# The block scale of x computed by GpSimd, directly ahead of its multiplication by the reciprocal

## The chip, the cores and the metric

The kernel runs on one core of a Trainium2 chip. The metric is the device time of one execution in microseconds (us), as a median over runs of the same kernel. Five engines work side by side and wait for one another only through semaphores: TensorE (PE in the profile, its weight loads PEld), VectorE (DVE), ScalarE (ACT), GpSimd (POOL) and the queue that issues DMAs (SP). Each engine works through its own list of instructions in order, and an instruction that waits holds up all that stand behind it on that engine.

## What is computed

A layer of attention with rotary positions and a decay mask, then a gated feed-forward part whose inputs and weights are quantised to FP4 in blocks of 16 values, each part with a residual and a layer norm. The part on which the change bears is the quantisation:

```python
def fp4_quant_dequant(x):
    xb = x.reshape(shape[:-1] + (shape[-1] // BLOCK, BLOCK))      # BLOCK = 16
    scale = jnp.max(jnp.abs(xb), axis=-1, keepdims=True) / 6.0
    scale = jnp.maximum(scale, jnp.float32(1e-12))
    xn = xb / scale
    idx = jnp.searchsorted(_MID, jnp.abs(xn))
    q = _GRID[idx] * jnp.sign(xn) * scale
    return q.reshape(shape)
...
x = _layernorm(x + attention(x), axis=-1)
gate = fp4_linear(x, w_gate); y = fp4_linear(x, w_up)
h = silu(gate) * y
x = _layernorm(x + fp4_linear(h, w_down), axis=-1)
```

x is 8 batches of 1024 rows of 256, so a row has 16 blocks. Everything is float32.

## The kernel before

**Tiles and steps.** The 8 x 1024 rows are 64 tiles of 128 rows. After an opening written out by hand, a loop runs `step(s)` for s = 3 to 62, and a closing part is written out by hand again. Every engine has its own `step`, with its own order. Step s works on several tiles at once, one stage apart: `now` = s (scores and softmax), `prev` = s - 1 (attention output, first norm, quantisation of x up to `x_units`), `gu` = s - 2 (rest of the quantisation of x, then gate and up product), `dn` = s - 3 (gated unit, quantisation of h), `fin` = s - 4 (down product), `end` = s - 5 (second norm, output). Nothing schedules this at build time: the order in the text of each `step` is the order on the engine.

**Five kinds of step.** Each batch b has 8 steps (s = 8b + j), and the branches of `step` follow what is done for the next batch on top of the tile's work. A *rotation step* (j = 0, and 2, 4, 6 while there is a next batch) has TensorE project queries or keys into the PSUM tile `ps_g` (`project_next`). A *values step* (j = 3) and the *urgent step* (j = 7) project the values. A *plain step* (j = 1 and 5) has no projection. The steps 57 to 62 are those of the *last block*, with nothing for a next batch. Over the steps 3 to 62 there are 7 urgent, 7 values, 13 plain, 27 rotation steps and 6 of the last block. Urgent steps are followed by a rotation step, plain steps too, values steps too.

**The quantisation of x.** For tile i, `x_max` (L1588, VectorE) writes the largest magnitude of each block into row 2 of the small tile `xsc`; `x_scales` (L1595, VectorE) makes the scale from it in row 0; `x_reciprocals` (L1600, VectorE) writes the reciprocal in row 1; `x_units` (L2068, GpSimd) multiplies the 256 columns of x by it; ScalarE takes magnitudes (`x_magnitude`), VectorE rounds (`x_shift`, `x_grid`), GpSimd multiplies by the scale (`x_quantised`), TensorE transposes (`x1_transposes`). Helpers hold the instruction itself, so the profile shows L1454 for `x_max`, L1459 for `x_scales`, L1463 for `x_reciprocals` and L2019 for all multiplications by a scale.

**What stands around it.** On VectorE, behind `x_reciprocals(prev)`: `second_residual(fin)` (L1586) in the urgent and plain steps, then `h_low(dn, 0)` and `h_low(dn, 1)` (L1518, L1521), then the next step's `gated` and `silu` (L1468, L1479) of two thirds of the gated unit. On GpSimd, ahead of `x_units(prev)`: both halves of `decay_half(now)` (L2116) in the urgent and values steps; the first half only, with the second behind, in the plain steps and those of the last block; and none, with `h_quantised(dn, 1)` (L2019) ahead, in the rotation steps. Behind it come the copies of the rotated queries or keys (`rotated_low`, L2033 and L2035) in the urgent and plain steps.

**What TensorE waits for.** `prob_transposes(prev, g)` needs the decayed half and `htl_done` of `h_low` two steps of the pipeline back (the tile whose `h_low` ran in the step before). `project_next` and `values_next` wait, in `projection()`, until the last `silu` of tile `dn` is done (`h_done`), since `ps_g` holds that tile's gate and up product. `values_product_first(prev)` needs `probs_low(prev, 0)` (L1529).

Of the kernel before, what the change touches and what calls it, by code (L numbers as in the profile page):

```python
# [7 lines left out]
ALU = mybir.AluOpType  # L8
# [28 lines left out]
TIES_DOWN = 1.0 + 2.0 ** -22  # L37
MIN_SCALE = 1e-12
# [26 lines left out]
def live(i):  # L65

    return 0 <= i < TILES


def wait(eng, sem, value):  # L70

    if value > 0:
        eng.wait_ge(sem, value)
# [34 lines left out]
def build(nc, x, xt, wq, wk, wv, wg, wu, wd, decay, rope, ident_in, out):  # L108
# [4 lines left out]
    with ExitStack() as ctx:  # L113
# [1229 lines left out]
        def _(dve):  # L1343
# [248 lines left out]
                    wait(dve, xq_done, i)  # L1592
                    block_max(x1[:, i % 4, :], xsc, xmax_done)

            def x_scales(i):  # L1595
                if live(i):
                    wait(dve, xmax_done, i + 1)
                    block_scales(xsc, xscale_done)

            def x_reciprocals(i):  # L1600
                if live(i):
                    wait(dve, xscale_done, i + 1)
# [118 lines left out]
            weight_low(7)  # L1721
            x_max(0)
            weight_low(8)
            x_scales(0)
            x_reciprocals(0)
            row_max(2)
            probs_low(1, 0)
# [8 lines left out]
            silu(0, 0)  # L1736
            first_norm(1)
            x_max(1)
            x_scales(1)
            x_reciprocals(1)  # L1740

            def step(s):
                now, prev, gu, dn, fin = (s - lag for lag in range(5))
                rot, c_v = rotation(s), values_chunk(s)
                if rot is not None:
# [18 lines left out]
                    row_max(now)  # L1764
                    first_norm(prev)
                    x_max(prev)
                    x_scales(prev)
                    x_reciprocals(prev)
                    gated(gu, 0)
                    second_residual(fin)  # L1770
# [3 lines left out]
                elif c_v is not None and rotation_is_urgent(s):  # L1774
# [20 lines left out]
                    first_norm(prev)  # L1795
                    silu(gu, 0)
                    x_max(prev)
                    x_scales(prev)
                    x_reciprocals(prev)
                    second_residual(fin)  # L1800
                    h_low(dn, 0)
# [1 line left out]
                elif c_v is not None:  # L1803
                    if s > OPEN:
                        x_shift(gu)
                    row_inverse(prev)
                    gated(dn, 1)
                    gated(dn, 2)
                    silu(dn, 1)
                    silu(dn, 2)  # L1810
                    if s == OPEN:
                        x_shift(gu)
                    x_grid(gu)
                    probs_low(prev, 0)
                    h_max(dn)
                    h_scales(dn)
                    h_reciprocals(dn)
                    probs_low(prev, 1)
                    v_low(c_v, 0)
                    xqt_low(gu)  # L1820
                    v_low(c_v, 1)
                    h_shift(dn)
                    h_grid(dn)
                    first_residual(prev)
                    row_max(now)
                    gated(gu, 0)
                    silu(gu, 0)
                    first_norm(prev)
                    second_residual(fin)
                    x_max(prev)  # L1830
                    x_scales(prev)
                    x_reciprocals(prev)
                    h_low(dn, 0)
                    h_low(dn, 1)
                elif s // NT == NB - 1:
                    gated(dn, 1)
                    gated(dn, 2)
                    silu(dn, 1)
                    silu(dn, 2)
                    x_shift(gu)  # L1840
                    h_max(dn)
                    probs_low(prev, 0)
                    h_scales(dn)
                    x_grid(gu)
                    h_reciprocals(dn)
                    probs_low(prev, 1)
                    row_max(now)
                    xqt_low(gu)
                    row_inverse(prev)
                    first_residual(prev)  # L1850
                    h_shift(dn)
                    h_grid(dn)
                    gated(gu, 0)
                    first_norm(prev)
                    x_max(prev)
                    x_scales(prev)
                    silu(gu, 0)
                    second_residual(fin)
                    x_reciprocals(prev)
                    h_low(dn, 0)  # L1860
                    h_low(dn, 1)
                else:
                    gated(dn, 1)
                    silu(dn, 1)
                    row_inverse(prev)
                    x_shift(gu)
                    gated(dn, 2)
                    x_grid(gu)
                    silu(dn, 2)
                    h_max(dn)  # L1870
                    probs_low(prev, 0)
                    h_scales(dn)
                    h_reciprocals(dn)
                    probs_low(prev, 1)
                    xqt_low(gu)
                    row_max(now)
                    first_residual(prev)
                    h_shift(dn)
                    h_grid(dn)
                    first_norm(prev)  # L1880
                    x_max(prev)
                    gated(gu, 0)
                    x_scales(prev)
                    silu(gu, 0)
                    x_reciprocals(prev)
                    second_residual(fin)
                    h_low(dn, 0)
                    h_low(dn, 1)
# [23 lines left out]
            x_max(last - 1)  # L1912
            gated(last - 2, 0)
            silu(last - 2, 0)
            x_scales(last - 1)
            x_reciprocals(last - 1)
            row_inverse(last)
            h_low(last - 3, 0)
# [15 lines left out]
            last_moments_of(0, r1, (r1_done, TILES))  # L1934
            last_first_norm()
            x_max(last)
            x_scales(last)
            x_reciprocals(last)
            h_shift(last - 2)
            h_grid(last - 2)  # L1940
# [35 lines left out]
        def _(pool):  # L1976
# [86 lines left out]
            def x_quantised(i):  # L2063
                if live(i):
                    wait(pool, xgrid_done, i + 1)
                    times_scale(xv[:], xv[:], xsc, 0).then_inc(xq_done, 1)

            def x_units(i):  # L2068
                if live(i):
                    wait(pool, xinv_done, i + 1)  # L2070

                    wait(pool, xqt_done, i)
                    if i == 0:
                        pool.wait_ge(wquant_done, 3)
                    times_scale(xv[:], x1[:, i % 4, :], xsc, 1).then_inc(xn_done, 1)
# [92 lines left out]
            r1_variance(0)  # L2168
            r1_inverse(0)
            new_x_low(2)  # L2170
            x_units(0)
            rotated_low(0, 1)
            x_quantised(0)
# [1 line left out]
            decay_half(2, 1)  # L2175
            r1_variance(1)
            r1_inverse(1)
            x_units(1)
            rotate(1, 2, 0)

            def step(s):
                now, prev, gu, dn, fin, end = (s - lag for lag in range(6))
                rot, turned, c_v, c_x = rotation(s), rotation(s - 1), values_chunk(s), split_chunk(s)
                if rot is not None:
# [8 lines left out]
                    h_quantised(dn, 0)  # L2193
                    h_copied(dn)
                    h_quantised(dn, 1)
                    x_units(prev)
                    decay_half(now, 0)
                    decay_half(now, 1)
                elif c_v is not None and rotation_is_urgent(s):
# [10 lines left out]
                    r1_inverse(prev)  # L2210
                    decay_half(now, 0)
                    decay_half(now, 1)
                    x_units(prev)
                    rotated_low(*turned)
                elif c_v is not None:
# [11 lines left out]
                    r1_inverse(prev)  # L2227
                    decay_half(now, 0)
                    decay_half(now, 1)
                    x_units(prev)  # L2230
                elif s // NT == NB - 1:
                    r2_variance(end)
# [9 lines left out]
                    h_copied(dn)  # L2242
                    h_quantised(dn, 1)
                    decay_half(now, 0)
                    x_units(prev)
                    decay_half(now, 1)
                    if turned is not None:
                        rotated_low(*turned)
                else:
# [12 lines left out]
                    h_quantised(dn, 0)  # L2262
                    h_quantised(dn, 1)
                    decay_half(now, 0)
                    x_units(prev)
                    decay_half(now, 1)
                    if turned is not None:
# [14 lines left out]
            h_quantised(last - 3, 1)  # L2282
            r2_shift(last - 5)
            decay_half(last, 0)
            x_units(last - 1)
            decay_half(last, 1)
            x_quantised(last - 1)
            h_units(last - 2)
            last_inverse(0)
            x_units(last)  # L2290
            r2_variance(last - 4)
            r2_inverse(last - 4)
# [76 lines left out]
```

## Time and profile before

| | |
|---|---|
| median of 3 runs | 1030.45 us (1030.28 to 1030.70) |
| span of the profiled execution | 1028.9 us |
| granted TensorE clock | 1.00 |
| busy: PE, PEld, DVE, ACT, POOL | 98%, 89%, 87%, 57%, 73% of the span |
| `x_scales` on VectorE | 64 instructions, 26.9 us in all |
| `x_reciprocals` | 64 instructions, 15.9 us in all |
| `x_units` on GpSimd | 64 instructions, 39.9 us in all |

The span runs from the first to the last instruction of one execution; the runs' median is 1.55 us above it. A share of busy time is an average over stages with different limits; which wait ends last at a given place is read from the timeline of that place.

In a timeline row the columns are: start and duration in us, engine, line, operation, output<-input, shapes, number of instructions merged into the row, and in brackets the engine's idle time ahead of it with the engine and instruction that ended it. A row of two merged instructions has one start and the duration of both.

### The profile page before, as it was taken

To read this page: it belongs to the slowest core of one execution; us is meant where nothing else is said; L and a number is where in the kernel's file an instruction comes from. 1 tells how busy PE (TensorE), PEld (TensorE's weight loads), DVE (VectorE), ACT (ScalarE), POOL (GpSimd) and SP (SyncE) were. 2 spreads that over 40 slices of the span, in tenths; PEclk is the share of its full clock that TensorE was granted. 3 is DMA by queue.
4 is the path that set the end of the run, shared out by engine and by line. 5 is a ranking of instruction groups with operands and counts; after the bars stand their busy time and mean duration, and the time that the engine had idled before them with its cause. 6 is when DMAs were issued, how large, how long until landed. Compare 5 with 4: busy or idle time off the path is not lost.

```text
span 1028.9 us, 20101 instructions
## 1 busy us (share of the span) xinstructions
PE 1009.9 (98%) x6490; PEld 917.9 (89%) x6490; DVE 894.9 (87%) x1876; ACT 582.5 (57%) x1451; POOL 752.7 (73%) x973
## 2 busy tenths in 40 slices
PE   8899999999999999999999999999999999999996
PEld 7788999999999999999999999999999999989885
DVE  7989988888888889898888988889888888988886
ACT  3655556655665655655565665566556565565543
POOL 5977868776786867778687686876768686776654
PEclk9999999999999999999999999999999999999999
DMA  8020111110120101201020010211112020000000
GB/s 304 11 68 7 62 41 54 42 62 12 42 82 12 62 22 33 82 21 58 16 83 32 22 62 17 78 42 25 49 41 79 15 63 17 17 21 22 21 11 26
DMA packets 28263, 47.23 MB, mean 46 GB/s; under 512 B 2816, under 2 KB 21504, under 8 KB 26240
## 3 DMA queue, kind: packets, MB, share of 16 engines
q1 hardware_dynamic: 27472, 44.90, 13.8%
q8 instruction: 53, 0.87, 0.4%
q10 hardware_dynamic: 688, 1.05, 0.3%
q14 instruction: 50, 0.41, 0.1%
HBM read 37.55 MB, written 8.39 MB: 45 GB/s over the span
## 4 chain that ended last, share of the span: by engine, by line
PE 85%; POOL 5%; DVE 5%; issue 4%; DMA 1%; ACT 0%; SPq 0%; POOLq 0%; DVEq 0%; ACTq 0%
PE ps_g L491 11%; PE ps_g L492 11%; PE ps_g L493 11%; PE ps_oy L491 9%; PE ps_oy L493 9%; PE ps_oy L492 9%; PE ps_t L500 9%; PE ps_s L491 5%; PE ps_s L492 5%; PE ps_s L493 5%; POOL h L2019 2%; PE ps_oy L500 1%; DMA first_gate_up<-w_up 1%; PE ps_oy L677 1%; PE ps_oy L676 1%
## 5 line engine op out<-in xcount | busy, mean ns | idle before, releaser
L2019 POOL TENSOR_TENSOR h<-h,hsc 128x704 f32<-128x704 f32 x252 | 202.4, 815 | 58.8 <-DVE h L1511 28.5
L2116 POOL TENSOR_TENSOR prob<-prob,decay_t 128x512 f32<-128x512 f32 x128 | 163.6, 1292 | 4.0 <-ACT prob L1058 3.6
L491 PE MATMUL ps_oy<-v_h,pt_h 128*128 128x256 f32 x512 | 150.5, 294 | 0.0
L491 PE MATMUL ps_g<-wgu_h,xqt_h 128*128 128x480 f32 (+1 forms) x380 | 149.6, 394 | 0.4 <-DVE xqt_l L1548 0.3
L493 PE MATMUL ps_oy<-v_h,pt_l 128*128 128x256 f32 x512 | 144.8, 283 | 0.0
L492 PE MATMUL ps_oy<-v_l,pt_h 128*128 128x256 f32 x512 | 144.8, 283 | 0.0
L493 PE MATMUL ps_g<-wgu_h,xqt_l 128*128 128x480 f32 (+1 forms) x380 | 142.6, 375 | 0.0
L492 PE MATMUL ps_g<-wgu_l,xqt_h 128*128 128x480 f32 (+1 forms) x380 | 142.6, 375 | 0.0
L491 PE MATMUL ps_s<-k_h,q_h 128*128 128x512 f32 x256 | 104.8, 409 | 0.0
L491 PEld LDWEIGHTS ps_oy<-v_h,pt_h 128*128 128x128 f32 x512 | 97.7, 191 | 3.3 <-DVE pt_l L1529 1.7
L492 PE MATMUL ps_s<-k_l,q_h 128*128 128x512 f32 x256 | 100.6, 393 | 0.0
L493 PE MATMUL ps_s<-k_h,q_l 128*128 128x512 f32 x256 | 100.3, 392 | 0.0
L1007 ACT ACTIVATE th<-ps_g 128x240 f32<-128x240 f32 x188 | 68.1, 366 | 55.1 <-PE ps_g L493 52.3
L492 PEld LDWEIGHTS ps_oy<-v_l,pt_h 128*128 128x128 f32 x512 | 97.9, 191 | 1.4
L493 PEld LDWEIGHTS ps_oy<-v_h,pt_l 128*128 128x128 f32 x512 | 97.8, 191 | 0.0
L1015 ACT CAST pt_h<-ps_t 128x512 fp32r<-128x512 f32 x128 | 71.0, 589 | 38.2 <-PE ps_t L500 35.4
L1047 ACT CAST xqt_h<-ps_oy 128x256 fp32r<-128x256 f32 x63 | 23.6, 374 | 119.4 <-PE ps_oy L500 119.1
L1529 DVE TENSOR_TENSOR pt_l<-ps_t,pt_h 128x512 fp32r<-128x512 f32 x128 | 85.8, 671 | 5.1 <-ACT pt_h L1015 5.0
L491 PE MATMUL ps_oy<-wd_h,ht_h 128*128 128x256 f32 x315 | 89.1, 283 | 0.6 <-DVE ht_h L1521 0.6
L2025 POOL TENSOR_TENSOR rot_a<-rot_a,rot_b 128x512 f32<-128x512 f32 x58 | 75.0, 1294 | 19.6 <-DVE rot_b L1442 19.6
L493 PE MATMUL ps_oy<-wd_h,ht_l 128*128 128x256 f32 x315 | 89.2, 283 | 0.0
L492 PE MATMUL ps_oy<-wd_l,ht_h 128*128 128x256 f32 x315 | 89.2, 283 | 0.0
(260 smaller groups left out, 3053.7 us busy)
## 6 DMA issues: line engine op xcount, KB each, us to landing
rope_t<-rope SPq DMA_DIRECT2D x15, 1024.0 KB, 5.3
xres<-x SPq DMA_DIRECT2D x64, 128.0 KB, 2.0
out<-yout SPq DMA_DIRECT2D x63, 128.0 KB, 1.7
xin<-x_t SPq DMA_DIRECT2D x14, 512.0 KB, 4.1
first_rope<-rope SPq DMA_DIRECT2D x2, 512.0 KB, 8.4
decay_t<-decay SPq DMA_DIRECT2D x1, 960.0 KB, 12.2
first_down<-w_down SPq DMA_DIRECT2D x1, 704.0 KB, 10.3
first_gate_up<-w_gate SPq DMA_DIRECT2D x2, 256.0 KB, 7.8
```

The costliest lines, as they stand in the source:

```text
L491: pe.matmul(dst, a_h, b_h, start=(start and i == 0), stop=False)
L492: pe.matmul(dst, a_h, b_l, start=False, stop=False)
L493: mm = pe.matmul(dst, a_l, b_h, start=False, stop=(stop and i == n - 1))
L500: mm = pe.transpose(dst[:, i, 0:r], src, ident[0:r, 0:r])
L676: pe.matmul(ps_y[:, 0:D], ht_h[:, FC - 1, :], wd_h[:, FC - 1, :], start=False, stop=False)
L1007: nc.scalar.activation(th[:, part(r)], gate_up_at(i, r)[:, 0], ACT.Tanh, scale=0.5)\
L1015: nc.scalar.copy(pt_h[:, 4 * g:4 * g + 4, :], ps_t[:, g]).then_inc(pth_done, 1)
L1047: nc.scalar.copy(xqt_h[:], xqt_at(i)).then_inc(xqth_done, 1)
L1529: tt(pt_l[:, 4 * g:4 * g + 4, :], ps_t[:, g], pt_h[:, 4 * g:4 * g + 4, :].bitcast(F32), ALU.subtract).then_inc(ptl_done, 1)
L2019: return tt(blocks(dst), blocks(src), sc[:, which, at:at + n].unsqueeze(2).to_broadcast([P, n, QB]), ALU.mult)
L2025: tt(rot_a[:, a, :], rot_a[:, a, :], rot_b[:, 1 - a, :], ALU.add if a else ALU.subtract)\
L2116: tt(prob[:, keys], prob[:, keys], decay_t[:, lo:lo + CW], ALU.mult).then_inc(decayed, 1)
```

## The change

`x_scales(i)` moves from VectorE's program to GpSimd's. It becomes one `tensor_scalar` of 128 x 16 on GpSimd that waits for `xmax_done` and raises `xscale_done`. VectorE's `x_reciprocals` keeps its place behind `x_max` and still waits for `xscale_done`, which now comes from the other engine. On GpSimd the new instruction stands directly ahead of `x_units`, which waits for the reciprocal, in all 64 tiles. Nothing else is moved; TensorE's and ScalarE's lists are the same.

```diff
@@ VectorE
-            def x_scales(i):
-                if live(i):
-                    wait(dve, xmax_done, i + 1)
-                    block_scales(xsc, xscale_done)
-
             def x_reciprocals(i):
                 if live(i):
                     wait(dve, xscale_done, i + 1)
@@ VectorE, step, urgent branch (and the call taken out of every other branch)
                     x_max(prev)
-                    x_scales(prev)
                     x_reciprocals(prev)
@@ GpSimd
+            def x_scales(i):
+                if live(i):
+                    wait(pool, xmax_done, i + 1)
+                    nc.gpsimd.tensor_scalar(xsc[:, 0, :], xsc[:, 2, :], TIES_DOWN / 6.0, MIN_SCALE * TIES_DOWN, ALU.mult,
+                                            ALU.max).then_inc(xscale_done, 1)
+
@@ GpSimd, step, urgent branch (and ahead of x_units in every other branch)
                     decay_half(now, 0)
                     decay_half(now, 1)
+                    x_scales(prev)
                     x_units(prev)
                     rotated_low(*turned)
```

How the lists stand at two places. First the urgent step (s = 23). VectorE before; `xsc` is the tile of block scales, the row of L1459 is `x_scales`, and L1518 is `h_low`:

```order
L1454 TENSOR_REDUCE xsc<-x 128x16 [waits xq_done,x1_done]
L1459 TENSOR_SCALAR xsc<-xsc 128x16 [waits xmax_done]
L1463 RECIPROCAL xsc<-xsc 128x16 [waits xscale_done]
L1586 TENSOR_TENSOR r<-ps_oy,x 128x256 [waits y2_done,y_done]
L1518 TENSOR_TENSOR ht_l<-ps_t,ht_h 128x512 [waits hth_done]
```

VectorE in the changed kernel, same place:

```order
L1454 TENSOR_REDUCE xsc<-x 128x16 [waits xq_done,x1_done]
L1463 RECIPROCAL xsc<-xsc 128x16 [waits xscale_done]
L1586 TENSOR_TENSOR r<-ps_oy,x 128x256 [waits y2_done,y_done]
L1518 TENSOR_TENSOR ht_l<-ps_t,ht_h 128x512 [waits hth_done]
L1518 TENSOR_TENSOR ht_l<-ps_t,ht_h 128x128 [waits hth_done]
```

GpSimd in the changed kernel in the same step (`prob<-prob,decay_t` are the decay halves, `xv<-x,xsc` is `x_units`):

```order
L2081 TENSOR_TENSOR rs<-ve,mhalf 128x1 [waits x1_done,ve1_done]
L2108 TENSOR_TENSOR prob<-prob,decay_t 128x512 [waits exp_done] x2
L2057 TENSOR_SCALAR xsc<-xsc 128x16 [waits xmax_done]
L2005 TENSOR_TENSOR xv<-x,xsc 128x256 [waits xqt_done,xinv_done]
L2019 TENSOR_TENSOR k_l<-rot_a,k_h 128x512 [waits kqh_done]
```

The scale has gone from VectorE's list, and on GpSimd it stands behind both decay halves; VectorE's reciprocal, with everything behind it, waits for that place in GpSimd's list.

Second, GpSimd in a plain step (s = 25), before:

```order
L2019 TENSOR_TENSOR h<-h,hsc 128x192 [waits hcopy_done,hgrid_done]
L2116 TENSOR_TENSOR prob<-prob,decay_t 128x512 [waits exp_done]
L2019 TENSOR_TENSOR xv<-x,xsc 128x256 [waits xqt_done,xinv_done]
L2116 TENSOR_TENSOR prob<-prob,decay_t 128x512 [waits exp_done]
L2035 TENSOR_TENSOR q_l<-rot_a,q_h 128x1024 [waits kqh_done]
```

and in the changed kernel:

```order
L2005 TENSOR_TENSOR h<-h,hsc 128x192 [waits hcopy_done,hgrid_done]
L2108 TENSOR_TENSOR prob<-prob,decay_t 128x512 [waits exp_done]
L2057 TENSOR_SCALAR xsc<-xsc 128x16 [waits xmax_done]
L2005 TENSOR_TENSOR xv<-x,xsc 128x256 [waits xqt_done,xinv_done]
L2108 TENSOR_TENSOR prob<-prob,decay_t 128x512 [waits exp_done]
L2021 TENSOR_TENSOR q_l<-rot_a,q_h 128x1024 [waits kqh_done]
```

Here it stands behind the first decay half, and the second half has both the scale and the reciprocal's return ahead of it.

## Rows read from the trace of the kernel before

**Rows 1.** The page's first part: busy time of each engine

```profile
PE 1009.9 (98%) x6490; PEld 917.9 (89%) x6490; DVE 894.9 (87%) x1876; ACT 582.5 (57%) x1451; POOL 752.7 (73%) x973
```

**Rows 2.** Timeline, steps 23 and 24 (urgent, then rotation): DVE, POOL, PEld

```profile
385.83 0.26 DVE L1463 RECIPROCAL xsc<-xsc 128x16 f32<-128x16 f32 x1
...
386.27 0.87 DVE L1518 TENSOR_TENSOR ht_l<-ps_t,ht_h 128x512 fp32r<-128x512 f32 x2
...
386.96 0.63 POOL L2019 TENSOR_TENSOR xv<-x,xsc 128x256 f32<-128x256 f32 x1
...
388.11 0.70 DVE L1479 SCALAR_TENSOR_TENSOR h<-th,ps_g 128x240 f32<-128x240 f32 x2
...
388.99 0.19 PEld L491 LDWEIGHTS ps_g<-xt_h,wqkv_h 128*128 128x128 f32 x1
```

**Rows 3.** The tile view of xsc: count, shortest, median and longest duration (ns)

```profile
L1459 DVE TENSOR_SCALAR xsc<-xsc x64: 175/242/1267, 53.6 to 1000.0; 128x16 f32<-128x16 f32 x64
```

**Rows 4.** Timeline, a values step (s = 27): POOL and DVE

```profile
445.07 2.53 POOL L2116 TENSOR_TENSOR prob<-prob,decay_t 128x512 f32<-128x512 f32 x2
...
446.37 1.27 DVE L1459 TENSOR_SCALAR xsc<-xsc 128x16 f32<-128x16 f32 x1
```

**Rows 5.** Groups by line of POOL: busy us, mean ns of one, idle before

```profile
L2019 POOL TENSOR_TENSOR h<-h,hsc 128x64 f32<-128x64 f32 x63 | 18.5, 293 | 0.2 <-DVE h L1511 0.2
...
L2082 POOL TENSOR_SCALAR ve<-sq 128x1 f32<-128x1 f32 x63 | 12.0, 190 | 57.5 <-ACT ps_oy L1075 57.4
```

**Rows 6.** Timeline, a rotation step (s = 26): POOL

```profile
429.37 0.62 POOL L2019 TENSOR_TENSOR xv<-x,xsc 128x256 f32<-128x256 f32 x1 [0.40 <-DVE xsc L1463]
```

**Rows 7.** Timeline, steps 3 and 4: DVE, POOL, PEld

```profile
79.10 0.25 DVE L1463 RECIPROCAL xsc<-xsc 128x16 f32<-128x16 f32 x1
79.27 0.82 DVE L1518 TENSOR_TENSOR ht_l<-ps_t,ht_h 128x512 fp32r<-128x512 f32 x2
...
80.23 0.63 POOL L2019 TENSOR_TENSOR xv<-x,xsc 128x256 f32<-128x256 f32 x1
...
81.05 0.69 DVE L1479 SCALAR_TENSOR_TENSOR h<-th,ps_g 128x240 f32<-128x240 f32 x2
...
81.80 0.19 PEld L491 LDWEIGHTS ps_g<-xt_h,wqkv_h 128*128 128x128 f32 x1 [0.72 <-DVE h L1479]
```

**Rows 8.** Timeline, steps 25 and 26 (plain, then rotation): DVE, POOL, PEld

```profile
414.42 0.24 DVE L1463 RECIPROCAL xsc<-xsc 128x16 f32<-128x16 f32 x1
...
415.35 0.62 POOL L2019 TENSOR_TENSOR xv<-x,xsc 128x256 f32<-128x256 f32 x1
...
415.57 0.89 DVE L1518 TENSOR_TENSOR ht_l<-ps_t,ht_h 128x512 fp32r<-128x512 f32 x2 [0.64 <-ACT ht_h L1108]
...
417.42 0.69 DVE L1479 SCALAR_TENSOR_TENSOR h<-th,ps_g 128x240 f32<-128x240 f32 x2
...
418.30 0.19 PEld L491 LDWEIGHTS ps_g<-xt_h,wqkv_h 128*128 128x128 f32 x1
```

**Rows 9.** Timeline, the last block (steps 57, 59 and 60): DVE, POOL, PE

```profile
907.47 0.89 DVE L1518 TENSOR_TENSOR ht_l<-ps_t,ht_h 128x512 fp32r<-128x512 f32 x2 [0.34 <-ACT ht_h L1108]
...
933.44 0.23 DVE L1463 RECIPROCAL xsc<-xsc 128x16 f32<-128x16 f32 x1
...
934.70 0.63 POOL L2019 TENSOR_TENSOR xv<-x,xsc 128x256 f32<-128x256 f32 x1
...
934.73 0.89 DVE L1518 TENSOR_TENSOR ht_l<-ps_t,ht_h 128x512 fp32r<-128x512 f32 x2 [1.05 <-ACT ht_h L1108]
...
938.32 0.68 DVE L1529 TENSOR_TENSOR pt_l<-ps_t,pt_h 128x512 fp32r<-128x512 f32 x1
...
939.05 0.39 PE L491 MATMUL ps_oy<-v_h,pt_h 128*128 128x256 f32 x1
```

**Rows 10.** Waits of PE: us in total, times, longest

```profile
PE ps_t L500 <- POOL h L2019: 2.7, 5, 1.1
PE ps_oy L491 <- DVE ht_h L1521: 0.6, 1, 0.6
```

**Rows 11.** Busy time by stretch: PE, PEld, DVE, ACT, POOL, then granted clock

```profile
24.00:32.00 8.00, 5.31 (x34) 4.29 (x34) 7.58 (x15) 5.51 (x8) 7.29 (x6) 1.00 0.01 1
```

More of the change, by code:

```diff
@@ L1723, in _ @@
             weight_low(8)
-            x_scales(0)
             x_reciprocals(0)
@@ L1738, in _ @@
             x_max(1)
-            x_scales(1)
             x_reciprocals(1)
@@ L1797, in step @@
                     x_max(prev)
-                    x_scales(prev)
                     x_reciprocals(prev)
@@ L1830, in step @@
                     x_max(prev)
-                    x_scales(prev)
                     x_reciprocals(prev)
@@ L1855, in step @@
                     x_max(prev)
-                    x_scales(prev)
                     silu(gu, 0)
@@ L1882, in step @@
                     gated(gu, 0)
-                    x_scales(prev)
                     silu(gu, 0)
@@ L1914, in _ @@
             silu(last - 2, 0)
-            x_scales(last - 1)
             x_reciprocals(last - 1)
@@ L1936, in _ @@
             x_max(last)
-            x_scales(last)
             x_reciprocals(last)
@@ L2170, in _ @@
             new_x_low(2)
+            x_scales(0)
             x_units(0)
@@ L2177, in _ @@
             r1_inverse(1)
+            x_scales(1)
             x_units(1)
@@ L2212, in step @@
                     decay_half(now, 1)
+                    x_scales(prev)
                     x_units(prev)
@@ L2229, in step @@
                     decay_half(now, 1)
+                    x_scales(prev)
                     x_units(prev)
@@ L2244, in step @@
                     decay_half(now, 0)
+                    x_scales(prev)
                     x_units(prev)
@@ L2264, in step @@
                     decay_half(now, 0)
+                    x_scales(prev)
                     x_units(prev)
@@ L2284, in _ @@
             decay_half(last, 0)
+            x_scales(last - 1)
             x_units(last - 1)
@@ L2289, in _ @@
             last_inverse(0)
+            x_scales(last)
             x_units(last)
```

## The prediction, made before the changed kernel ran

> **What bounds the kernel now.** I read the page's busy line first [rows 1]: TensorE is busy for 1009.9 of 1028.9 us. VectorE has 87% and GpSimd 73%, so nothing gets faster by relieving them unless TensorE waits for them, and it hardly does: in the view of waits TensorE's largest single entry is 2.7 us for GpSimd, VectorE's largest after the opening 0.6 us [rows 10]. Any time that the change takes from TensorE is therefore lost for good, and little can be won. So I went to the timeline at the ends of the steps and asked, for each kind of step, how late the reciprocal comes and who is behind it.
>
> **What is removed.** VectorE loses 64 `tensor_scalar` of 128x16. They took 0.18 us at the shortest, 0.24 in the median and 1.27 at the longest [rows 3]. The long ones are holds: in a values step `x_scales` starts at 446.37 and ends at 447.64, 0.04 us behind the end of GpSimd's decay halves, 445.07 + 2.53 = 447.60 [rows 4]. The Trainium skill, "SBUF — State Buffer", § Who interferes with whom, says that a VectorE `tensor_scalar` in its fast mode and a GpSimd instruction exclude each other for the whole instruction; the trace agrees with that. By the rule alone the removal would hand all these holds back to VectorE.
>
> The rows say that it does not. The new instruction stands on GpSimd at the place where GpSimd comes free, so VectorE's reciprocal waits for the same end, and for a whole instruction more.
>
> **What is added.** One GpSimd `tensor_scalar` of 128x16 per tile, of which the trace has none. The nearest rows are the same operation on one column, 0.19 us, and a multiplication of 64 columns, 0.29 us [rows 5]. I take 0.21, near the first, since 16 columns are closer to 1 than to 64. The Trainium skill, "GPSIMD Engine Reference", § 4.1 Engine selection, puts elementwise work on VectorE, GpSimd being about 2x slower for two inputs; no run here shows this size. With twice VectorE's 0.24 the new instruction would cost 0.48, and the sum below would be some 9 us larger.
>
> The handover from GpSimd to VectorE is new. In the other direction it takes 0.08 (reciprocal's end to `x_units` at 429.37, whose 0.40 of idle time it ends [rows 6]); I take 0.04, between 0 and 0.08. So where GpSimd is busy until then, **the reciprocal starts 0.21 + 0.04 = 0.25 us behind the place where `x_units` starts now**.
>
> **Urgent step, 7 times.** `x_units` starts at 386.96, the reciprocal at 385.83 [rows 2]. It moves to 386.96 + 0.25 = 387.21, **1.38 later**. Behind it VectorE has no idle time: `h_low` at 386.27 follows back to back, and the two `silu` of the next step end at 388.11 + 0.70 = 388.81. They move to 390.19. TensorE's projection into `ps_g` waits for them; it starts at 388.99 now. How long that handover takes is seen at step 4, where TensorE does wait: the `silu` pair ends at 81.05 + 0.69 = 81.74 and the weight load starts at 81.80, 0.06 later [rows 7]. So the projection moves to 390.25, and TensorE loses 390.25 - 388.99 = **1.26 us**. The transposes ahead of it wait for `h_low` too, but for less, and inside the same delay. 7 x 1.26 = 8.8 us.
>
> **Plain step, 13 times.** The reciprocal goes from 414.42 to 415.35 + 0.25 = 415.60 [rows 8]. Here VectorE had 0.64 us idle ahead of `h_low`. In the urgent step `h_low` starts 0.44 behind the reciprocal with no idle time [rows 2]; so it now starts at 416.04 and not 415.57, 0.47 late. The `silu` pair ends at 418.11 + 0.47 = 418.58, the projection starts at 418.64 and not at 418.30: **0.34 us**, 13 x 0.34 = 4.4 us. The second decay half is behind the new instruction and the reciprocal (0.25 + 0.24 + 0.08 = 0.57 late). It is needed by the second group of transposes, just ahead of this projection; I cost it at nothing, since the projection's wait covers it.
>
> **Values step, 7 times.** In six of them VectorE is held already until GpSimd is free [rows 4], so the reciprocal is only some 0.14 later, and the projection of the next step loses 0 to 0.14: 0.5 us together. The seventh is step 3, where GpSimd is later: 79.10 to 80.23 + 0.25 = 80.48, 1.38 late, and the projection of step 4 is waiting for VectorE already [rows 7], so all of it counts: 1.4 us.
>
> **Rotation step, 27 times, and the opening.** GpSimd waits there with 0.40 us of idle time for the reciprocal [rows 6], so it comes free about when `x_scales` ends now, and the new path costs about 0.14. VectorE's next `h_low` waits for ScalarE in most of them and takes it up: 0. For the opening, and for the last tile, whose chain is all waits, I add 0.2.
>
> **Last block, tiles 56 to 62.** In step 59 the reciprocal goes from 933.44 to 934.70 + 0.25 = 934.95, 1.51 later. VectorE had 1.05 idle behind it: `h_low` starts 0.17 behind the reciprocal when nothing else holds it (79.10 and 79.27 [rows 7]), that is at 935.12, not 934.73, 0.39 late [rows 9]. From there VectorE works without a gap up to `probs_low`, which ends at 938.32 + 0.68 = 939.00, and TensorE's first values product starts at 939.05: it has no room. So 0.39 for each of the six tiles 57 to 62, 2.3 us. Behind tile 56 the idle time is only 0.34, 0.71 less, so 1.1 us.
>
> **The sum.** 8.8 + 4.4 + 0.5 + 1.4 + 0.2 + 2.3 + 1.1 = 18.7 us against the profiled span of 1028.9, that is 1047.6; the runs' median stands 1.55 above that span, so 1030.45 + 18.7 = **1049.2 us**, 1.8% slower. The term that I know least is the new instruction's duration. It counts in some 33 places (7 + 13 + 7 + 6), so each 0.1 us is 3.3 us: 0.19 gives 1048.5, 0.29 gives 1051.8. A handover of 0 or 0.08 moves it by 1.3 either way.
>
> **Rivals.**
> *Partly absorbed.* The late `silu` may be no full loss, if GpSimd, with VectorE's holds gone, comes to its place earlier, or if the transposes ahead of the projection (1 us of TensorE's list) slide too. Then the step 4 term (1.4) and the last block (3.4) stand, and nothing to half of the other 13.9: 4.8 to 11.8 us, 1035 to 1042, middle 1038. Against it: step 4 shows the projection waiting for exactly this `silu`, and what GpSimd does ahead of its place waits for ScalarE and for its own list, not for VectorE's scale.
> *Larger.* The new instruction costs 0.42 to 0.48 as VectorE's did with its holds, or late copies on GpSimd hold VectorE's remaining `tensor_scalar` elsewhere: 33 x 0.2 = 7 more, 1056 to 1063. A drop of the clock belongs here, but the row speaks against it: in the stretch 24 to 32 us TensorE was busy for 5.31 of 8 us only, and the granted clock stayed at 1.00, the 2.4 GHz level [rows 11].
> *Faster.* VectorE gets 26.9 us of its list back, holds among it. This decides if GpSimd reaches the new instruction before VectorE reaches the reciprocal, in more than a few places; then VectorE runs ahead and TensorE's waits for VectorE go. They are small [rows 10], so 1 to 2.5 us are to be had: 1028 to 1029. In the rows above GpSimd is the later one by 0.9 to 1.3 us everywhere but in the rotation steps.
> *No change.* TensorE's room is larger than the handovers suggest, and all delays end in VectorE's idle time: 1030.5.
>
> **Chances.** Forecast (1043 to 1054) 0.63, partly absorbed 0.14, larger 0.15, no change 0.05, faster 0.03. The range 1040 to 1058 holds the forecast, the lower part of the larger case and the upper end of the absorbed one, about 0.8. A measurement of this kernel can tell about 0.2%, 2 us, from no change. Faster by more than that 0.02, within it 0.06, slower 0.92.
>
> **What the profile after would show.** VectorE's reciprocal waits for GpSimd's `xsc`, some 1.9 us of idle time in urgent steps, in sum 40 us or more over the 64; GpSimd's `x_units` waits for the reciprocal in all 64 (about 0.4 each). TensorE's weight load of `ps_g` behind VectorE's `h` idles 1.2 us in the rotation steps that follow an urgent one and 0.3 behind a plain one; the first values product of the last block waits for `pt_l`. The rest of each step is unchanged in length. I am wrong if TensorE's idle time grows by much less than 18 us, if it stands ahead of other instructions, or if the new instruction takes other than 0.19 to 0.29 us.

## The result and the profile after

The changed kernel takes **1055.84 us** (1055.47 to 1055.88), against 1030.58 for the kernel before in the same comparison: a ratio of 1.0246, 95% interval 1.0234 to 1.0258, slower. Forecast were 1049.2 us, 18.7 more than before, with a range of 1040 to 1058. Sign and range hold; the sum is 6.6 us short. The spans of the two profiled executions are 1053.8 and 1028.9, so 24.9 us are to be found in the trace. The granted TensorE clock is 1.00 again, so the time is waiting and not a slower clock.

The page of the kernel after, busy line, chain of work that ended last by engine, and granted clock:

```profile
PE 1023.0 (97%) x6490; PEld 917.0 (87%) x6490; DVE 865.3 (82%) x1812; ACT 586.0 (56%) x1451; POOL 771.6 (73%) x1037
...
POOL 35%; PE 28%; issue 19%; DVE 14%; ACT 3%; POOLq 0%; ACTq 0%; DVEq 0%
...
PEclk9999999999999999999999999999999999999999
```

and the chain in the page of the kernel before:

```profile
PE 85%; POOL 5%; DVE 5%; issue 4%; DMA 1%; ACT 0%; SPq 0%; POOLq 0%; DVEq 0%; ACTq 0%
```

VectorE has 64 instructions and 29.6 us less than in [rows 1]; GpSimd has 64 instructions and 18.9 us more. By busy time this looks like a good trade: the work got cheaper in sum. The chain says what it did to the path. Followed back from the last instruction, the time before was TensorE's for 85% of the span, which is what a kernel bound by TensorE looks like. Now GpSimd, VectorE and "issue" (waiting for nothing that the profile shows) hold 68% of it: at the end of an urgent or a plain step the chain goes through GpSimd's decay, the new instruction and VectorE's list.

The tile view of `xsc` (duration in ns: shortest/median/longest), then the waits of all engines (us in total, times, longest), then TensorE's own:

```profile
L2057 POOL TENSOR_SCALAR xsc<-xsc x64: 273/273/278, 53.7 to 1024.9; 128x16 f32<-128x16 f32 x64
L1463 DVE RECIPROCAL xsc<-xsc x64: 252/253/256, 54.1 to 1025.2; 128x16 f32<-128x16 f32 x64
```

```profile
DVE xsc L1463 <- POOL xsc L2057: 78.0, 64, 2.2
...
POOL xv L2005 <- DVE xsc L1463: 23.8, 64, 0.4
```

```profile
PE ps_g L491 <- DVE h L1479: 5.2, 9, 0.6
PE ps_t L500 <- DVE ht_l L1518: 3.7, 9, 1.1
```

The scale takes 0.273 us in every place, where VectorE's took 0.175 to 1.267 [rows 3]. The first line of waits is new and large: VectorE now sits 78 us behind GpSimd's scale, with 26.9 us of work taken from it. TensorE's two grown waits, for `silu` (`h`) and for `h_low` (`ht_l`), add up to 8.9 us only. That view is of its matmuls; the waits of its weight loads, which stand idle first, show nearly the whole loss:

```profile
PEld ps_g L491 <- DVE h L1479: 13.2, 28, 0.9
PEld ps_t L500 <- issue: 7.3, 9, 1.5
PEld ps_t L500 <- POOL prob L2108: 5.9, 20, 1.1
```

In the kernel before these three were 1.0, 0.4 and 1.1 us, so they grew by 23.9 us. Which of them decides in a given step the sums don't tell; for that the timeline has to be laid beside the one before.

**An urgent step.** Timeline of the kernel after, steps 23 and 24, GpSimd, VectorE and TensorE's weight loads; it answers to [rows 2]:

```profile
392.47 2.55 POOL L2108 TENSOR_TENSOR prob<-prob,decay_t 128x512 f32<-128x512 f32 x2 [0.52 <-ACT prob L1058]
395.10 0.27 POOL L2057 TENSOR_SCALAR xsc<-xsc 128x16 f32<-128x16 f32 x1
395.41 0.25 DVE L1463 RECIPROCAL xsc<-xsc 128x16 f32<-128x16 f32 x1 [2.24 <-POOL xsc L2057]
395.86 0.87 DVE L1518 TENSOR_TENSOR ht_l<-ps_t,ht_h 128x512 fp32r<-128x512 f32 x2
...
396.65 0.92 PEld L500 LDWEIGHTS ps_t<-ident_sb,prob 128*128 128x128 f32 x8 [0.69 <-issue]
...
397.69 0.69 DVE L1479 SCALAR_TENSOR_TENSOR h<-th,ps_g 128x240 f32<-128x240 f32 x2
398.44 0.19 PEld L491 LDWEIGHTS ps_g<-xt_h,wqkv_h 128*128 128x128 f32 x1 [0.86 <-DVE h L1479]
```

VectorE stood idle for 2.24 us ahead of the reciprocal and was released by the scale. From the reciprocal's start to the projection are 398.44 - 395.41 = 3.03 us; in [rows 2], with the 0.06 handover, they are 388.81 + 0.06 - 385.83 = 3.04. So everything behind the reciprocal moved rigidly, as forecast. What is off is where the reciprocal starts. The decay halves end at 392.47 + 2.55 = 395.02 and the scale starts at 395.10, 0.08 **behind** that end; the reciprocal starts 0.39 behind it. The forecast had the scale start where `x_units` did, which was 0.05 **ahead** of that end (386.96 [rows 2] against 384.46 + 2.55 = 387.01):

```profile
384.46 2.55 POOL L2116 TENSOR_TENSOR prob<-prob,decay_t 128x512 f32<-128x512 f32 x2 [0.52 <-ACT prob L1058]
```

**A plain step, and the last block.** The same of steps 25 and 26, which answers to [rows 8], and of steps 59 and 60 with TensorE's products, which answers to [rows 9]:

```profile
423.54 1.27 POOL L2108 TENSOR_TENSOR prob<-prob,decay_t 128x512 f32<-128x512 f32 x1
424.89 0.28 POOL L2057 TENSOR_SCALAR xsc<-xsc 128x16 f32<-128x16 f32 x1
425.20 0.26 DVE L1463 RECIPROCAL xsc<-xsc 128x16 f32<-128x16 f32 x1 [1.59 <-POOL xsc L2057]
425.65 0.88 DVE L1518 TENSOR_TENSOR ht_l<-ps_t,ht_h 128x512 fp32r<-128x512 f32 x2
...
428.23 0.19 PEld L491 LDWEIGHTS ps_g<-xt_h,wqkv_h 128*128 128x128 f32 x1 [0.34 <-DVE h L1479]
```

```profile
957.28 0.25 DVE L1463 RECIPROCAL xsc<-xsc 128x16 f32<-128x16 f32 x1 [1.89 <-POOL xsc L2057]
...
960.97 0.68 DVE L1529 TENSOR_TENSOR pt_l<-ps_t,pt_h 128x512 fp32r<-128x512 f32 x1
961.70 0.39 PE L491 MATMUL ps_oy<-v_h,pt_h 128*128 128x256 f32 x1
```

`h_low` had 0.64 us idle ahead of it in [rows 8] and has none now; it follows the reciprocal by 0.45, and the projection waits for `silu`. The second decay half, now at 426.12, ends at 427.42, and TensorE's second group of transposes starts 0.05 behind that; on this path alone the projection would have come 0.14 late. The `silu` ends last and makes it 0.51. In the last block the first values product starts 0.05 behind the end of `pt_l` (960.97 + 0.68 = 961.65), as it did in [rows 9], but later in the step.

**The ledger.** For each step I took the time from TensorE's first weight load to its first of the next step, and subtracted that of the kernel before. Such differences add up to the difference of the spans, and TensorE's list is the same in all kernels, so each is time that TensorE lost in that step. In us:

| steps | count | forecast, each | after, each | after, sum |
|---|---|---|---|---|
| rotation behind urgent | 7 | 1.26 | 1.41 to 1.48 | 10.08 |
| rotation behind plain | 13 | 0.34 | 0.52 to 0.57 | 7.05 |
| step 4, behind the first values step | 1 | 1.4 | 1.51 | 1.51 |
| the others behind values | 6 | 0.08 | 0.29 to 0.32 | 1.83 |
| last block, steps 58 to 62 | 5 | 1.1, then 0.39 | 0.94, 0.50, 0.49, 0.51, 1.03 | 3.47 |
| step 3 (values), closing part | | 0.2, and 0.39 for each of the last two of the six tiles | 0.17, 0.78 | 0.95 |
| sum | | 18.7 | | 24.9 |

The rotation steps are 0.15 to 0.24 us over their forecast each (step 4 by 0.11), steps 59 to 61 by 0.1, and step 58 is 0.16 under it. No other step lost more than 0.01 us: the plain and urgent steps themselves are at 0.00. The pattern of the forecast is right, and a quantity that enters in the 33 places is too small.

Step 62 holds two of the places. Its own values product is 0.51 late, like those of steps 59 to 61; the other 0.51 lies at its end, where the closing part opens with the transposes of tile 62, which wait for the `h_low` that stands behind the reciprocal of tile 61:

```profile
1000.17 0.42 PEld L500 LDWEIGHTS ps_t<-ident_sb,prob 128*128 128x128 f32 x4 [0.96 <-issue]
```

The same load had 0.44 us of idle time before.

### The profile page after: what moved, and what is told of

Same layout as the page of the kernel before. It is cut to its first block, busy times and chain, and to the rows that moved or that the text cites. A ratio compares the mean times of both kernels' runs of the same rounds, so it can differ in the third digit from the quotient of the medians.

```text
span 1053.8 us, 20101 instructions
## 1 busy us (share of the span) xinstructions
PE 1023.0 (97%) x6490; PEld 917.0 (87%) x6490; DVE 865.3 (82%) x1812; ACT 586.0 (56%) x1451; POOL 771.6 (73%) x1037
## 4 chain that ended last, share of the span: by engine, by line
POOL 35%; PE 28%; issue 19%; DVE 14%; ACT 3%; POOLq 0%; ACTq 0%; DVEq 0%
POOL h L2005 9%; POOL prob L2108 8%; PE ps_g L491 4%; PE ps_g L493 4%; PE ps_g L492 4%; POOL xt_l L2027 3%; POOL xv L2005 3%; PE ps_oy L493 3%; PE ps_oy L491 3%; PE ps_oy L492 3%; DVE ht_l L1518 2%; POOL rot_a L2011 2%; POOL rs L2095 2%; POOL rs L2081 2%; PE ps_t L500 2%
```

## The experiments

Two theories. **Place:** what costs is that the scale stands behind GpSimd's decay, so that VectorE's list waits for GpSimd's; where GpSimd is free in time it costs nothing. The 6 us too much are its duration and start (0.19 us in 33 places). **Rivals:** the instruction's own time on a GpSimd that is busy for 73% costs anywhere; or the loss is the hold between the two engines; or the missing 6 us are some other delay, such as `x_units` and what follows it.

### The scale on GpSimd in the rotation steps only

VectorE keeps its `x_scales` at the place of before for the 37 other tiles. `kind(i)` is the kind of step in which tile i is quantised.

```
 # VectorE, at its places of before
+    if live(i) and kind(i) not in ON_POOL:      # ON_POOL = ("rotation",)
 # GpSimd
-    if live(i):
+    if live(i) and kind(i) in ON_POOL:
```

> The scale is computed by GpSimd in the 27 rotation steps only, where GpSimd is free when the maximum is ready and waits for the reciprocal anyway; in all other tiles VectorE computes it as before. Theory (what costs is the place in GpSimd's queue, behind a decay half): no measurable change, 1030.5 to 1032. Rival (the instruction and its two handovers cost wherever they stand, 25.3 us / 64 = 0.40 each): 27 x 0.40 = 10.7 more, about 1041.

Measured: 1031.05 us, ratio 1.0006 (0.9996 to 1.0015), and 0.33 us more by the ledger. The tile view of `xsc` and the waits of this kernel:

```profile
L2087 POOL TENSOR_SCALAR xsc<-xsc x27: 273/273/278, 92.4 to 891.6; 128x16 f32<-128x16 f32 x27
```

```profile
DVE xsc L1479 <- POOL xsc L2087: 15.9, 27, 0.6
```

VectorE waits all 27 times, 0.6 us each, and TensorE loses nothing that can be told from the noise. In step 26 the reciprocal starts 1.01 us behind the start of `x_max`, against 0.69 before the change, so it is 0.32 late, and so is the first third of `silu` behind it. TensorE's next load that waits for that `silu` stood 0.49 behind its end before, and had this room to give. So 27 of the 64 cost nothing, and at these places the instruction's own time on GpSimd has no price.

### In the urgent steps only

The same edit with `ON_POOL = ("urgent",)`.

> The scale is computed by GpSimd in the 7 urgent steps only, at the changed kernel's place behind both decay halves; in all other tiles by VectorE as before. Theory (TensorE loses the time in the rotation step behind each, place by place, and the places add): 7 x 1.43 = 10.0 us more than the kernel before, 1040.5. Rival (a delay is made good elsewhere, or the places depend on one another): less than 1037.

Measured: 1041.03 us, ratio 1.0103 (1.0088 to 1.0118). By the ledger six steps lose 1.43 to 1.47 each, as in the kernel after (1.41 to 1.48), and one (step 16) 1.79, which is not explained. The seven add up to 10.47; the opening was 0.39 shorter in this execution, which gives 10.1 for the whole. The waits:

```profile
DVE xsc L1479 <- POOL xsc L2087: 15.7, 7, 2.2
...
PE ps_g L507 <- DVE h L1495: 4.8, 8, 0.6
```

Seven instructions hold 10 of the 25 us. The terms add up: a step's price does not depend on what the other steps do.

### The scale one decay half earlier on GpSimd

```
-decay_half(now, 1)        # urgent and values; in plain steps
 x_scales(prev)            # and the last block decay_half(now, 0),
+decay_half(now, 1)        # in the closing part decay_half(last, 0)
```

> As changed, but on GpSimd the scale stands one decay half earlier: ahead of the first half in plain steps and those of the last block, between the halves in urgent and values steps. All 64 scales stay on GpSimd. Theory (place in the queue): the reciprocal in a plain step then starts about 0.1 later than before the change, and in an urgent step about 0.3; TensorE loses some 0.15 in each of the 7 rotation steps behind an urgent one and 0.3 at step 4, together with the closing part 1.5 to 3 us: 1032 to 1034. Rival (cost of the instruction and handovers wherever they stand): 1050 or more. Second rival (the decay halves, pushed back by 0.35, now hold the transposes): 1036 to 1040.

Measured: 1034.25 us, ratio 1.0037 (1.0022 to 1.0052); by the ledger 2.67: urgent places 0.16 to 0.23 each, step 4 0.27, step 58 0.47, closing part 0.53, values steps 0.18, all others 0.00. The runs' median is 3.8 above before, 1.1 more than the ledger of the one profiled execution. That execution was the fastest of the four, with a granted clock of 1.000 and a span of 1031.6; two had 0.999 and 1032.1 and 1032.2, and the slowest 0.997 and 1033.5. So the rest goes together with a lower clock; where in the kernel it fell, no trace shows. The median is a quarter of a microsecond above the theory's 1032 to 1034. Timeline of an urgent step, GpSimd and VectorE:

```profile
385.28 1.30 POOL L2108 TENSOR_TENSOR prob<-prob,decay_t 128x512 f32<-128x512 f32 x1 [0.52 <-ACT prob L1058]
386.66 0.27 POOL L2057 TENSOR_SCALAR xsc<-xsc 128x16 f32<-128x16 f32 x1
386.96 0.25 DVE L1463 RECIPROCAL xsc<-xsc 128x16 f32<-128x16 f32 x1 [0.98 <-POOL xsc L2057]
```

```profile
DVE xsc L1463 <- POOL xsc L2057: 36.4, 64, 1.0
```

Same instruction, same 64 times, same engine; the reciprocal starts 1.25 us earlier against the decay, and 22 of the 25 us are gone. VectorE still waits 36.4 us in sum, which costs almost nothing. This is the run that tells the place from the instruction. It is also the answer to the hold: with the scale on GpSimd there is no VectorE scale to hold in either kernel, and the time differs by 21.6 us.

### The scale as a product of two tiles

`tensor_scalar` replaced by `tensor_tensor` with a tile of the constant 1/6 (times the rounding factor). The clamp at the smallest scale is left out.

```
-nc.gpsimd.tensor_scalar(xsc[:, 0, :], xsc[:, 2, :], TIES_DOWN / 6.0,
-                        MIN_SCALE * TIES_DOWN, ALU.mult, ALU.max)
+tt(xsc[:, 0, :], xsc[:, 2, :], sixth[:], ALU.mult)
```

> As changed, but GpSimd's instruction is a tensor_tensor (times a tile that holds the factor) and not a tensor_scalar with two operations; the clamp at the smallest scale is left out. In the trace of the changed kernel the tensor_scalar takes 0.27 us and starts 0.08 behind the end of the decay half, while a tensor_tensor behind another starts 0.04 ahead of its end. Theory (the size that the prediction missed is this start gap and the duration, 0.19 us in some 33 places): the instruction takes about 0.21, starts 0.12 earlier, and the kernel is 5 to 6.5 us faster than the changed one, 1049.5 to 1051. Rival (the missing 6.6 us come from elsewhere, from GpSimd's later copies or VectorE's holds): 1054 or more.

Measured: 1049.65 us, ratio 1.0189 (1.0174 to 1.0204), and 18.73 by the ledger, close to the prediction's 18.7 (that the hundredths agree is luck: the opening took 0.28 more and the last block 0.5 less than forecast). Rotation steps lose 1.24 to 1.28 behind urgent (forecast 1.26) and 0.34 to 0.39 behind plain (0.34), the others behind values 0.08 to 0.12 (0.08). GpSimd's timeline in an urgent step and the tile view:

```profile
390.71 2.55 POOL L2111 TENSOR_TENSOR prob<-prob,decay_t 128x512 f32<-128x512 f32 x2 [0.52 <-ACT prob L1060]
393.21 0.23 POOL L2061 TENSOR_TENSOR xsc<-xsc,sixth 128x16 f32<-128x16 f32 x1
```

```profile
L2061 POOL TENSOR_TENSOR xsc<-xsc,sixth x64: 215/222/235, 54.0 to 1018.7; 128x16 f32<-128x16 f32 x64
```

This instruction starts at 393.21, 0.05 ahead of the end of the decay (390.71 + 2.55 = 393.26), and takes 0.222. That is what the forecast had assumed (0.05 ahead, 0.21), and the time is what it said. So the mechanism with its 33 places was right, and 6.2 of the 6.6 us go with the start and duration of `tensor_scalar`: 0.13 + 0.05 us in 33 places are 5.9.

### The scale issued twice

```
+nc.gpsimd.tensor_scalar(xdup[:, 0:D // QB], xsc[:, 2, :], TIES_DOWN / 6.0,
+                        MIN_SCALE * TIES_DOWN, ALU.mult, ALU.max)
 nc.gpsimd.tensor_scalar(xsc[:, 0, :], xsc[:, 2, :], ...)
```

> As changed, with GpSimd's instruction issued twice in each tile, the first time into a tile that nobody reads. Theory (each 0.1 us ahead of the reciprocal counts in some 33 places): if the second one takes 0.27 and starts right behind, 0.3 x 33 = 9 to 10 us more than the changed kernel, plus a few tenths where the room of other steps is used up: 1065 to 1068. Rival (a delay is partly absorbed, or counts in all 64 places): 1060, or 1073 and more.

Measured: 1075.74 us, ratio 1.0442 (1.0425 to 1.0460); by the ledger 42.06, 17.1 more than the kernel after. The theory's 1065 to 1068 was too low, and the number lies in the rival's "1073 and more". By the runs' medians it is 19.9 more: the profiled execution (1072.87, granted clock 0.999) was the fastest of the four, and two at 0.995 took 1076.6 and 1076.7. Timeline of the urgent step, and of the middle of a rotation step:

```profile
398.00 2.54 POOL L2111 TENSOR_TENSOR prob<-prob,decay_t 128x512 f32<-128x512 f32 x2 [0.52 <-ACT prob L1059]
400.62 0.28 POOL L2058 TENSOR_SCALAR xdup<-xsc 128x16 f32<-128x16 f32 x1
400.96 0.27 POOL L2060 TENSOR_SCALAR xsc<-xsc 128x16 f32<-128x16 f32 x1
401.27 0.25 DVE L1464 RECIPROCAL xsc<-xsc 128x16 f32<-128x16 f32 x1 [2.57 <-POOL xsc L2060]
404.30 0.19 PEld L492 LDWEIGHTS ps_g<-xt_h,wqkv_h 128*128 128x128 f32 x1 [0.86 <-DVE h L1480]
...
415.73 0.25 DVE L1464 RECIPROCAL xsc<-xsc 128x16 f32<-128x16 f32 x1 [0.93 <-POOL xsc L2060]
416.49 0.39 DVE L1480 SCALAR_TENSOR_TENSOR h<-th,ps_g 128x240 f32<-128x240 f32 x1
417.00 0.19 PEld L492 LDWEIGHTS ps_g<-wgu_h,xqt_h 128*128 128x128 f32 x1 [0.33 <-issue]
```

The second instruction delays the reciprocal by 0.34 (0.27 and 0.06 between the two), which in 33 places is 11 us, as foretold. The other 6 of the ledger's 17.1 come from the rotation steps, which lost 0.50 to 0.52 more behind each kind and not 0.34. In them a second place opened: the first third of `silu` of the next tile stands behind the reciprocal, ends at 416.88, and TensorE's next gate-and-up weight load starts 0.12 later, having idled 0.33 us, 0.29 more than before. Between that end and the load there were 0.49 us before and 0.16 in the kernel after, of which the handover needs 0.12, so only some 0.04 were left; two `tensor_scalar` use them up. TensorE makes good 0.11 of the 0.29 at the next load, and 0.18 stay. 33 x 0.35 + 27 x 0.18 = 16.4, against 17.1 by the ledger. So a delay now counts in the 27 rotation steps too, which is near the rival's "in all 64 places". The cover that made the rotation run free is finite, and the kernel after stands some 0.04 us from its edge.

### VectorE's reciprocal behind `h_low`

GpSimd as in the kernel after; in the urgent and values steps of VectorE:

```
-x_reciprocals(prev)
 ...
 h_low(dn, 1)
+x_reciprocals(prev)
```

> As changed, with GpSimd's list untouched, but in urgent and values steps VectorE's reciprocal stands behind h_low and not ahead of it. Theory (what costs there is VectorE's queue behind the waiting reciprocal, not GpSimd's own lateness): the losses of 10.1 us behind urgent steps and most of the 3.3 us at steps 4, 12, 20 and so on go, 1042 to 1044. Rival (GpSimd's later x_units and copies cost the time): no change from 1055.8, or slower.

Measured: 1043.36 us, ratio 1.0124 (1.0107 to 1.0141), by the ledger 12.9: the steps behind urgent fall from 1.45 to between 0.05 and 0.08, those behind values to 0.00 (step 4 to 0.49), and plain and last block stay (0.51 to 0.55; 0.94, 0.50, 0.51, 0.51, 1.03). Timeline of VectorE in an urgent step:

```profile
389.42 0.68 DVE L1518 TENSOR_TENSOR ht_l<-ps_t,ht_h 128x512 fp32r<-128x512 f32 x1
390.55 0.29 DVE L1521 TENSOR_TENSOR ht_h<-ps_t,ht_h 64x128 fp32r<-64x128 f32 x1
391.41 0.25 DVE L1463 RECIPROCAL xsc<-xsc 128x16 f32<-128x16 f32 x1 [0.56 <-POOL xsc L2057]
```

GpSimd is as late as in the kernel after and the scale is where it was; only what queues behind the waiting reciprocal has changed: VectorE now does `h_low` while it would have waited. 12 of the 25 us go. So the loss passes through VectorE's order (`h_low`, `silu` behind the reciprocal), and not through `x_units` and the quantisation that follows, which come as late as there (`x_units` 0.73 us behind the end of the decay, against 0.72).

### Both together

The scale one decay half earlier, and the reciprocal behind `h_low` in the urgent steps.

> Both repairs: on GpSimd the scale one decay half earlier in all steps, and in urgent steps VectorE's reciprocal behind h_low. Theory: the 1.3 us that the earlier place leaves behind the urgent steps go too, about 1.3 us faster than with the earlier place alone, 1032.5 to 1033; the losses at step 4, at step 58 and in the closing part stay, so it does not beat the kernel before. Rival (VectorE, with 27 us less to do, lets TensorE run ahead in the last block): 1029 or less.

Measured: 1032.36 us, ratio 1.0019 (1.0010 to 1.0029): the seven urgent places are at 0.00, and step 4, the values steps and step 58 are as in the earlier-half run. The closing part cost 2.09 us in the profiled execution, against 0.53 in the earlier-half run. Here the granted clock fell, to the 1.2 GHz level for some 3.4 us (stretch, busy time of PE, PEld, DVE, ACT and POOL, granted clock):

```profile
1004.00:1008.00 4.00, 2.37 (x19) 1.93 (x18) 3.39 (x11) 1.67 (x5) 2.51 (x6) 1.00 0.10 33
1008.00:1012.00 4.00, 4.00 (x14) 4.00 (x15) 2.81 (x7) 0.52 (x3) 1.39 (x1) 0.57 0.00 0
```

TensorE had been busy for 2.37 of the 4 us before it fell. An estimate from the second row: 0.43 of 4 us, 1.7 us, are lost, which is the difference. This execution took 1034.46 us, the nine others 1032.06 to 1032.76, so the 2.09 is not the kernel's usual closing part. The kernel is the best of the kernels with all 64 scales on GpSimd, 23 us below the kernel after, and it is not faster than before. No version tried beats the kernel before.

## Why the prediction was right, and where it was short

**What bounds the kernel: right.** TensorE had no slack to give, and all that was lost is lost in its list. Taking 26.9 us from VectorE gave nothing back: no step is shorter than before in any line of the ledger.

**The hold: right.** VectorE's 1.27 us scales [rows 4] are gone and the time of those steps did not fall; the reciprocal waits for the same end of GpSimd's list. The Trainium skill's rule ("SBUF — State Buffer", § Who interferes with whom) agrees with the hold in the trace of the kernel before, which ended 0.04 us behind GpSimd's decay [rows 4], and its removal won nothing here, because the wait that replaced it has the same release plus an instruction.

**The start of the reciprocal: this is the term that was too small.** The prediction said that "the reciprocal starts 0.21 + 0.04 = 0.25 us behind the place where `x_units` starts now". It takes 0.44: the start is 0.13 later than where a `tensor_tensor` would start (0.08 behind the decay's end and not 0.05 ahead of it), the duration is 0.273 and not 0.21 (0.06), and the handover of 0.04 was right (395.37 to 395.41). That is 0.19 in 33 places, 6.3 us, and 18.7 + 6.3 = 25.0 against 24.9 measured. (The sum itself has seven places in the last block and the count of 33 only six; with 34 it would be 25.2.) The duration was bounded from both sides, 0.19 to 0.29, and is inside its bounds. The start was not given a bound at all, since I took it over from an instruction of another kind. The trace of the kernel before had it; GpSimd's timeline ahead of its statistics:

```profile
388.79 1.30 POOL L2033 TENSOR_TENSOR k_l<-rot_a,k_h 128x512 fp32r<-128x512 f32 x1
390.18 0.19 POOL L2096 TENSOR_SCALAR ve<-sq 128x1 f32<-128x1 f32 x1
```

388.79 + 1.30 = 390.09, and `ve` starts 0.09 behind it. In all 45 places of that trace where a `tensor_scalar` stood directly behind a `tensor_tensor` on GpSimd, the gap was 0.08 us.

**Twice VectorE's duration: not borne out.** It would have been 0.48; at 16 columns GpSimd's instruction took 0.273, which is 0.03 over VectorE's median of 0.242 and 1.6 times its shortest, 0.175 [rows 3]. The Trainium skill, "GPSIMD Engine Reference", § 4.1 Engine selection, gives the factor of about 2 for two inputs and calls one input roughly line-rate. The scale reads one tile, so the prediction had applied the factor where it does not belong.

**Urgent steps: right but for that term.** 1.26 + 0.19 = 1.45, measured 1.41 to 1.48. One detail was foretold otherwise: TensorE idles in two pieces, 0.69 ahead of the transposes and 0.86 ahead of the projection, and not 1.2 in one. The prediction had called the first a wait "inside the same delay", which it is.

**Plain steps: right but for that term.** 0.34 + 0.19 = 0.53, measured 0.52 to 0.57. Costing the late second decay half at nothing held: on its own it would have made the projection 0.14 late in step 26, and `silu` made it 0.51 late. The kernel with `tensor_tensor` has it late too, and lost 0.34 to 0.39.

**Values steps.** Step 4 was forecast at 1.4 and lost 1.51; the other six at 0 to 0.14 each and lost 0.31 each. The 0.14 by which the reciprocal was to be late and the missing 0.19 make 0.33, so these steps had hardly any room, and the 0.5 us for all of them was too low for that reason too.

**Rotation steps at nothing: the cost right, the reason not.** The first run shows the cost. The prediction had the reciprocal 0.14 late there and `h_low`'s wait for ScalarE taking it up. It came 0.32 late. Before the change `h_low` waits for at most 0.05 us in these 27 steps, and its start moved from 1.19 to 1.07 behind the reciprocal, so it took up 0.12; in step 26 the rest went into VectorE's next wait for ScalarE, which shrank from 0.47 to 0.28 us. The least room is on a path that the prediction never looked at: TensorE's load behind the first third of `silu`, 0.49 less the handover of 0.12. It was enough by some 0.04 us, so that these steps stayed free is luck.

**Last block.** 1.1 and six times 0.39 were forecast for steps 58 to 62 and the closing part. The places behind the reciprocals of tiles 57 to 61 lost 0.49 to 0.52 each (steps 59 to 61, and twice in step 62). That is 0.07 less than 0.39 + 0.19 = 0.58, because the pair of `h_low` takes 0.89 us in [rows 9] and 0.82 when it follows the reciprocal at once (957.45 in step 59). Step 58 took 0.94 and the closing part 0.78; these two I leave open. The block's sum, 4.25 against 3.4 + 6 x 0.19 = 4.5, agrees.

**The rivals.** *Partly absorbed* fell: GpSimd did not come earlier, and each late `silu` ahead of a projection was a full loss. *Larger* had the right sign for the miss, but neither of its reasons: not a duration of 0.42 or more, not late copies, and the clock stayed at the 2.4 GHz level through stalls of up to 1.5 us (step 4) until 1.3 us before the end. *Faster* and *no change* fell with the measured time. The chain's 35% for GpSimd was not among the signs that I named, and would have been the clearest one.

## What to carry to other kernels

A small instruction moved to an idler engine takes over that engine's place in time: what it costs is how much later that queue reaches it, plus start, duration and handover, for everything that queues behind its consumer. Where the place is bad, the instruction's own time counts in full: an estimate from the 0.44 us by which the reciprocal starts behind the old place of `x_units`, in 33 places, is 14.5 of the 25 us, and a second copy cost another 17. Where there is room, all of it is free, until the room is used up. The same 64 instructions cost 25.3 us behind the decay, 3.8 one decay half earlier, and 27 of them nothing that can be told from the noise (0.6) in the rotation steps. When a start is taken from the trace, take it from an instruction of the same kind behind the same kind of predecessor, for a tenth of a microsecond counts as often as the place recurs.

## What the runs showed of the hardware

On GpSimd a `tensor_scalar` starts 0.08 us behind the end of a `tensor_tensor` and 0.06 behind another `tensor_scalar`. A `tensor_tensor` starts 0.04 to 0.05 ahead of the recorded end of a `tensor_tensor` before it, but 0.08 behind a `tensor_scalar` (in the kernel before, 260.27 + 0.19 and then 260.54). With 16 columns the two-operation `tensor_scalar` takes 0.273 us and the `tensor_tensor` 0.222, so here the form with two input tiles is the cheaper one, by 0.18 us with the start, or 6.2 us in this kernel (1055.84 against 1049.65; the latter without the clamp). GpSimd's result reaches VectorE in 0.04 us, where the other direction takes 0.08 [rows 6].
